# Cross-attention in a Perceiver layer: lower context parts made batch by batch, and the odd batches' query blocks formed one pair earlier

## The reference, cut to what matters

```python
# x (32, 32, 512) after a layer norm, y = ctx_768 (32, 257, 384), 16 heads of d = 32
q = (x @ Wq.T).reshape(B, N, H, d).transpose(0, 2, 1, 3)
kv = (y @ Wkv.T).reshape(B, N2, 2, H, d).transpose(2, 0, 3, 1, 4)
k, v = (kv[0], kv[1])
attn = jnp.einsum('bhnd,bhmd->bhnm', q * scale, k)
attn = jnp.where(pad_mask[:, None, :, None], attn, -1e9)
out = jnp.einsum('bhnm,bhmd->bhnd', softmax(attn), v)
```

## Time and profile before

| what | value |
|---|---|
| three executions | 1918.14, 1919.16, 1923.44 us (median 1919.16) |
| the profiled execution | 1923.16 us, of which 1921.4 us are the span from the first to the last instruction |
| busy share of the span | TensorE 81%, VectorE 62%, ScalarE 37%, GpSimd 5% |
| mean granted TensorE clock | 0.903 of full speed |
| the cross-attention's loops and ends (`attend`) | from 55.5 us to about 502 us of the span |

### The profile page before, as it was taken

The page is one execution under the profiler, slowest core; times in us unless marked ns, Lnnn a source line. Parts: engine busy times, 40 slices in busy tenths (PEclk is TensorE's granted clock), DMA queues, the critical chain, the costliest instruction groups (busy, mean ns, idle before and its releaser), DMA issues. The chain is left out here.

```text
span 1921.4 us, 22239 instructions
## 1 busy us (share of the span) xinstructions
PE 1551.8 (81%) x7255; PEld 1150.9 (60%) x7255; DVE 1198.6 (62%) x2627; ACT 711.2 (37%) x1361; POOL 94.7 (5%) x261
## 2 busy tenths in 40 slices
PE   7999999999799999229300079569999999999998
PEld 3888888888677777103100078546666666666664
DVE  4366556655422977999999746445565555555555
ACT  2333333333244454201000222134555555555552
POOL 0000000000000000003111200030000000000003
PEclk9999999999799999659755569679999999999999
DMA  3211011100214513540100132074515505235104
GB/s 116 77 34 33 16 33 33 33 16 16 66 52 67 93 61 32 92 154 22 44 0 0 45 87 50 1 279 175 184 58 203 195 19 203 105 121 178 37 17 137
DMA packets 116152, 152.93 MB, mean 80 GB/s; under 512 B 47072, under 2 KB 67936, under 8 KB 116064
## 3 DMA queue, kind: packets, MB, share of 16 engines
q1 hardware_dynamic: 110336, 137.68, 24.1%
q0 software_dynamic: 2560, 8.39, 1.3%
q10 hardware_dynamic: 3168, 5.77, 0.8%
HBM read 250.25 MB, written 31.33 MB: 147 GB/s over the span
## 5 line engine op out<-in xcount | busy, mean ns | idle before, releaser
L1674 DVE TENSOR_TENSOR gl<-w_gu,gh 128x2048 fp32r<-128x2048 f32 x138 | 290.8, 2107 | 16.3 <-ACT gh L1609 16.2
L1609 ACT CAST gh<-w_gu 128x2048 fp32r<-128x2048 f32 x138 | 242.3, 1756 | 60.9 <-DMA w_gu<-in_up_proj 50.9
L1564 PE MATMUL bank<-w_d,hT 128*128 128x512 f32 x506 | 244.0, 601 | 11.7 <-ACT hT L1633 11.7
L1541 PE MATMUL bank<-gh,xh 128*128 128x512 f32 (+1 forms) x552 | 219.4, 397 | 11.6 <-DVE xl L1665 9.8
L1707 DVE TENSOR_TENSOR hid<-silu,bank 128x256 f32<-128x256 f32 x138 | 55.1, 399 | 262.6 <-ACT silu L1622 262.6
L1543 PE MATMUL bank<-gh,xl 128*128 128x512 f32 (+1 forms) x552 | 207.4, 376 | 0.0
L1542 PE MATMUL bank<-gl,xh 128*128 128x512 f32 (+1 forms) x552 | 207.2, 375 | 0.0
L1170 PE MATMUL bank<-o_v,xnT 128*128 128x64 f32 x256 | 36.1, 310 | 178.7 <-DMA o_v<-scratch_v_rows 178.7
L1564 PEld LDWEIGHTS bank<-w_d,hT 128*128 128x128 f32 x506 | 92.1, 190 | 86.1 <-issue 55.8
L1170 PEld LDWEIGHTS bank<-o_v,xnT 128*128 128x128 f32 x256 | 35.8, 227 | 179.5 <-DMA o_v<-scratch_v_rows 179.5
L1622 ACT ACTIVATE silu<-bank 128x256 f32<-128x256 f32 x138 | 50.5, 366 | 212.7 <-PE bank L1543 212.7
(11 more groups left out here) (293 smaller groups left out, 3073.1 us busy)
## 6 DMA issues: line engine op xcount, KB each, us to landing
w_gu<-in_gate_proj SPq DMA_DIRECT2D x46, 1024.0 KB
w_gu<-in_up_proj SPq DMA_DIRECT2D x46, 1024.0 KB
w_d<-in_down_proj SPq DMA_DIRECT2D x46, 1024.0 KB
w_gu<-in_gate_proj SPq DMA_DIRECT2D x23, 768.0 KB
w_gu<-in_up_proj SPq DMA_DIRECT2D x23, 768.0 KB
w_d<-in_down_proj SPq DMA_DIRECT2D x23, 768.0 KB
ctx_raw<-in_ctxT SPq DMA_DIRECT2D x32, 385.5 KB, 3.8
scratch_gram<-gram SPq DMA_DIRECT2D x8, 768.0 KB, 3.5
```

Of the source, the lines that this page charges most:

```text
L1541: pe.matmul(bank, xh[s % 2][:, k, :], hi, start=(k == 0), stop=False)
L1564: mm = pe.matmul(bank, hT[n % 2][:, c, :], w_d[:, b * (BLK // P) + c, :], start=(b == 0 and c == 0), stop=(b == NB - 1 and c == cs[-1]))
L1609: nc.scalar.copy(gh[n % RING][:, :, :, 0:bw].rearrange("p k a f -> p (k a) f"), w_gu[:, :, :, b * BLK:b * BLK + bw].rearrange("p k a f -> ...
L1674: nc.vector.tensor_tensor(gl[n % RING][:, :, :, 0:bw].rearrange("p k a f -> p (k a) f"), w_gu[:, :, :, b * BLK:b * BLK + bw].rearrange("p ...
```

## The change

The lower part of a pair's context is made by two instructions of half the size, one for each batch, and `lo_done` counts batches. The first stands where the whole one stood; the second stands between `maxima` and `take_out` of the even batch. The waits on `lo_done` are rewritten to match: the keys need both halves, the values of a batch its own, a load both. The query blocks of the odd batch are formed one pair ahead, in the odd half of the pair before, between `take_turned` and `maxima`, in the half in which TensorE projects the keys; those of batch 1 are formed ahead of the first maxima.

```diff
--- before.py
+++ after.py
@@ -271,9 +271,9 @@
         def split_hi(act, s):
             nc.scalar.copy(ctx_hi[s][:, :, :, :], raw[:, :, :, 0:M - 1].rearrange("p a k m -> p k a m")).then_inc(hi_done, 1)
 
-        def split_lo(s):
-            nc.vector.tensor_tensor(ctx_lo[s][:, :, :, :], raw[:, :, :, 0:M - 1].rearrange("p a k m -> p k a m"),
-                                    ctx_hi[s][:, :, :, :].bitcast(F32), ALU.subtract).then_inc(lo_done, 1)
+        def split_lo(s, a):
+            nc.vector.tensor_tensor(ctx_lo[s][:, :, a, :], raw[:, a, :, 0:M - 1], ctx_hi[s][:, :, a, :].bitcast(F32),
+                                    ALU.subtract).then_inc(lo_done, 1)
 
 
         q_done, q_copied = sem("q_done"), sem("q_copied")
@@ -316,7 +316,8 @@
                         dve.wait_ge(wkv_split, 1)
                         nc.vector.tensor_tensor(wkv_lo[:, :, :], wkv[:, :, :], wkv_hi[:, :, :].bitcast(F32), ALU.subtract).then_inc(wkv_split, 1)
                         dve.wait_ge(hi_done, 1)
-                        split_lo(0)
+                        split_lo(0, 0)
+                        split_lo(0, 1)
                 nc.vector.tensor_reduce(same_token[:, :], ident[:, :].rearrange("p (h n) -> p n h", n=N), AX.X, ALU.add)
                 dve.wait_ge(vl_done, 1)
                 nc.vector.tensor_copy(v_last[:, :, :].rearrange("p c b -> p (c b)"), ps[7][:, 0:KC * B]).then_inc(vl_copied, 1)
@@ -357,7 +358,7 @@
             def _(sp):
                 load_first_weights(sp)
                 for j in range(1, B // 2):
-                    sp.wait_ge(lo_done, j)
+                    sp.wait_ge(lo_done, 2 * j)
                     load_context(sp, j)
 
             @block.tensor
@@ -372,7 +373,7 @@
                     return mm
 
                 def keys(j, s):
-                    pe.wait_ge(lo_done, j + 1)
+                    pe.wait_ge(lo_done, 2 * j + 2)
                     for c in range(KC):
                         if not first(j):
                             pe.wait_ge(exp_done, (j * 2 - 1) * KC + c + 1)
@@ -382,7 +383,7 @@
                               ).then_inc(k_done, 1)
 
                 def values(b, j, s):
-                    pe.wait_ge(lo_done, j + 1)
+                    pe.wait_ge(lo_done, b + 1)
                     if not (isinstance(b, int) and b < 2):
                         pe.wait_ge(t_copied, (b - 1) * 3)
                     for m in range(2):
@@ -549,9 +550,13 @@
                     nc.vector.tensor_reduce(oT[:, :, place * N:(place + 1) * N], o_masked[:, :, :, :].rearrange("p c h n -> p c n h"),
                                             AX.X, ALU.add).then_inc(o_taken, 1)
 
-                def ahead(b, s, slot):
+                def ahead(b, s, slot, split=None, spread=None):
                     take_turned(b, s)
+                    if spread is not None:
+                        spread_queries(spread, 1)
                     maxima(b + 1, 1 - s)
+                    if split is not None:
+                        split_lo(split, 1)
                     take_out(b, 2 * slot + s)
                     normalize(b + 1, 1 - s)
 
@@ -563,18 +568,18 @@
                     nc.vector.bn_stats(stats[:, bass.ds(t, 1), :].rearrange("p a c -> p (a c)"), x_tile)
 
                 def pair_ahead(j, slot, last=False, tile=None):
-                    spread_queries(j * 2 + 1, 1)
                     if not last:
                         dve.wait_ge(hi_done, j + 2)
-                        split_lo(1 - slot)
+                        split_lo(1 - slot, 0)
                     if tile is not None:
                         take_residual(tile)
-                    ahead(j * 2, 0, slot)
+                    ahead(j * 2, 0, slot, split=None if last else 1 - slot)
                     if not last:
                         spread_queries(j * 2 + 2, 0)
-                        ahead(j * 2 + 1, 1, slot)
+                        ahead(j * 2 + 1, 1, slot, spread=j * 2 + 3)
 
                 spread_queries(0, 0)
+                spread_queries(1, 1)
                 maxima(0, 0)
                 normalize(0, 0)
                 pair_ahead(0, 0)
```

## The result

The changed kernel takes 1901.73 us (median of 6 runs, 1899.77 to 1902.41), the kernel before 1919.12 (6 runs): a ratio of 0.9905, 95% interval 0.9894 to 0.9915, 17.4 us less. Forecast were 1900.9 us and 18.3 us less. Measured twice more, the ratio is 0.9894 (0.9878 to 0.9911) and 0.9897 (0.9877 to 0.9916), 20.9 and 19.9 us less. The profiled execution took 1900.15 us.

A forecast was written before the change was run, and what follows sets the result against it. TensorE was taken to set the pace, its apply held by VectorE's order: 15 waits cost 21.3 us, 3.0 stay, 18.3 saved from 1919.16 gives 1900.9 us. Range: some 2 us below 1897.9 to nearly 1910.

The forecast's parts named there:

- The bound and the place of the wait: Cross-attention: TensorE sets the pace; in even halves query blocks and lower part on VectorE delay the copies, holding apply.
- the rival of a change without effect: VectorE's order is not what holds apply, so the time stays at 1919; chance 1%.
- The control: Last pair, with no lower part: transposes to apply take 2.90 us without a wait, taken as floor without a tile.
- No other partner of TensorE took the wait's place: Rival: ScalarE's copies of the values hold TensorE in the same place instead, 1914 to 1919 us; chance 4%.
- The half's cost: Half the lower part on VectorE takes 0.87 us from start to start, bounds 0.84 and 1.67.
- costly halves: Rival: a half takes as long as the whole, only the query blocks' 9 us are won, 1910; chance 8%.
- four transposes are taken 0.63 us after their start, so it starts at 238.82: Even half with a tile: start of the residual's addition on VectorE, leading to apply at 241.79 and 1.37 us saved.
- the saving passes on whole behind the stage: Behind cross-attention only a weight load made at its start overlaps, so the full 18.3 us reach the program's time.
- The covers: Moved instructions and the later context load fit into idle time in both halves and on ScalarE; cost nothing.
- a rival that did not occur: Context load lands late, each us beyond 17 us costing one in 14 pairs; 1925 us at 19; chance 2%.

The follow-up runs named there:

- The single edits: Each edit alone against the kernel before: query blocks moved alone, 1909.13 us; lower part halved alone, 1905.47 us.
- e9_stats_behind_again: Repeat of the changed kernel with the residual tile's statistics moved behind the maxima and the second half: 1897.0 us, ratio 0.9884.

## Why the prediction was right

**The bound and the place of the wait** held. TensorE sets the pace, and two of VectorE's instructions ahead of the copies held apply. Taking each away is worth about its start-to-start time (in the tile halves 0.64 us for 0.60, and 0.80 for 0.80) until TensorE's own floor is reached. The single edits show both parts of that, and with them the rival of a change without effect falls. The granted clock stays at 1.00 in the loop.

**The control** held to 0.01 us: the last pair's 2.90 us is what every even half without a tile takes now. No other partner of TensorE took the wait's place, so that rival falls too.

**The half's cost.** 0.87 us was interpolated between two sizes, and 0.87 is measured. That the two sizes lie on a line, the prediction's argument against costly halves, was none, since any two do; the measured third size is what makes it one. The duration is 0.949, where the interpolation gave 0.955 and the Trainium skill's formula ("VectorE: DVE Perf Modes", in the section on the TRN2 errata) 0.957. The next instruction starts 0.08 to 0.09 us before the half ends, so the measured spacing decides, not the sum of durations. The prediction cites the section on the drain on the same page of the Trainium skill for the whole duration lying between starts. That section makes an exception of a next instruction that is not held, which starts earlier; the 0.08 to 0.09 us agree with the exception.

**The term that was mis-sized** is "four transposes are taken 0.63 us after their start, so it starts at 238.82". The 0.63 was the copies' distance; the residual's addition starts 0.74 us behind its transposes (231.71 to 232.45). It is 0.74 or 0.75 in all seven halves:

```profile
231.43 0.95 DVE L275 TENSOR_TENSOR ctx_lo<-ctx_raw,ctx_hi 128x768 fp32r<-128x768 f32 x1
232.45 0.69 DVE L566 TENSOR_TENSOR x_nat<-x_nat,bank 128x512 f32 x1
```

VectorE's queue is not the reason. In the kernel with the whole lower part behind the maxima VectorE stood idle before the addition:

```profile
234.45 0.60 PE L404 MATMUL bank<-ident,oT 128*128 128x128 f32 x4
```
```profile
235.19 0.69 DVE L565 TENSOR_TENSOR x_nat<-x_nat,bank 128x512 f32 x1 [0.95 <-PE bank L404]
```

0.74 again. It makes each tile half 0.10 us slower than forecast, 0.7 to 0.8 us in seven. From the first transposes to those of the last even batch the stage shrank by 410.01 - 392.56 = 17.45 us, for 18.3 forecast; this term is nearly all of the difference. Why the addition starts 0.11 us later than the copies do was not tried.

**Luck.** The three measurements, 17.4, 20.9 and 19.9 us less, lie further apart than the first does from the forecast of 18.3, so that it came within 1 us is luck. The stage gives 17.8; the three profiles of the changed kernel agree on it within 0.2 (410.0 to 410.2), and before there is one. Of the 17.8 0.34 us are not the forecast's: the last batch's apply takes 3.79 us before and 3.44 after. There the granted clock is 0.50 in the stretch from 498 to 500 us before, and 0.73 from 481 to 483 after, so it came back during apply. The prediction allowed for this in its range only. That the saving passes on whole behind the stage is not shown either way: the part behind it is told of in the last section.

**The covers** held where they were named: 0.77 us left in the odd half (0.75 forecast), 0.34 in the even one (0.28), the copy of the values still waiting for TensorE, the load with 12 us to spare. The price that was wrong belongs to a rival that did not occur: 4.5 us of lateness cost 2.8 us a pair, a part of it through the clock.

## What to carry to other kernels

Find the half or iteration in which the same wait does not occur (the last pair, the other parity): the distance between two instructions there is the floor, and the difference to it is what reordering can give. List what stands in the other engine's queue ahead of the awaited instruction and ask of each when its reader needs it; split an instruction where its readers come at different times. Edits that shorten one wait add up only until its floor is reached, and a piece moved too far turns into the next wait.

## What the runs showed that was not expected

The part of the program outside the stage is 1485 to 1494 us in the twelve profiles (span less stage). But for the first pair's lower part, halved or whole, and the place of batch 1's query blocks, it has the same instructions in all of them. The part behind L174 is 1411.8 to 1418.3 us. It is longest in the profile of the kernel before, and 1413.0, 1412.0 and 1412.7 in the three of the changed kernel. With one profile of the kernel before, no run here shows whether that is scatter or a part of the gain.

Some 4 us of scatter lie ahead of the stage, whose first transposes start at 73.1 to 77.3 us. The stretch from 50 to 60 us shows where, in the changed kernel's second profile and in that of e9_stats_behind_again:

```profile
50.00:60.00 10.00, 9.39 (x48) 8.05 (x48) 1.59 (x3) 1.40 (x4) 0.00 (x0) 0.83 0.55 193
```
```profile
50.00:60.00 10.00, 9.39 (x44) 8.61 (x44) 1.58 (x3) 0.27 (x1) 0.00 (x0) 0.58 0.19 63
```

TensorE is busy 9.39 us in both, but the granted clock (the number before the DMA's two) is 0.83 in one and 0.58 in the other. The stretch begins with small matmuls of 32 columns (L305), and the first projection behind them starts at 53.48 or at 56.77 us. So a single profile cannot show an edit of 3 us in its span; the distance between two instructions inside the touched stage repeats to 0.4 us.
